# Routing logits and mean as extra columns of the value and output projections, in a fused linear-attention and mixture-of-experts kernel

## The reference, cut to what matters

```python
x = x + attn(layernorm(x))            # qkv = x @ W_attn + b ; 16 heads of 8
#   q, k = elu(.) + 1 ; causal linear attention:
#   kv_t = kv_{t-1} + k_t v_t^T ; ksum_t = ksum_{t-1} + k_t
#   y_t = (q_t kv_t) / (q_t ksum_t + eps) ; attn = y @ W_proj + b_proj
z = layernorm(x)
logits = z @ Wr + br                  # 8 experts
top two experts per token, weights = softmax over those two
out = x + sum over the two: w_e * (relu(z @ W1[e] + b1[e]) @ W2[e] + b2[e])
```

## Time and profile before

| | us |
|---|---|
| median of 3 runs (344.52 to 345.48) | 345.19 |
| profiled execution | 345.68 |
| its span, first to last instruction | 343.9 |
| busy: PE, DVE | 289.6, 275.0 |
| busy: POOL, ACT | 248.5, 224.7 |

### The profile page before, as it was taken

One profiled execution on the slowest core, in us unless ns is written; L12 is line 12 of the kernel. 1 busy time (PEld: TensorE's weight loads), 2 busy tenths in 40 slices (PEclk: granted clock), 3 DMA queues, 4 the chain that ended last, 5 costly groups with the idle time before them and its releaser, 6 DMA issues.

```text
span 343.9 us, 7875 instructions
## 1 busy us (share of the span) xinstructions
PE 289.6 (84%) x2234; PEld 207.3 (60%) x2237; DVE 275.0 (80%) x623; ACT 224.7 (65%) x654; POOL 248.5 (72%) x252
## 2 busy tenths in 40 slices
PE   4798999989989999899695799999999999995000
PEld 4587855545545555555453577688888898884000
DVE  5888899999978987997999279986777777773096
ACT  2588721469989855555408896688888888882091
POOL 4648999659999998877775577777777777777200
PEclk9699999999999999999879699999999999999655
DMA  8991000000000001011110364516445645511497
GB/s 226 352 286 47 0 2 0 0 4 0 1 0 2 0 15 43 31 53 50 42 51 33 78 110 103 104 56 102 110 104 105 117 99 104 98 56 53 134 381 240
DMA packets 50026, 29.16 MB, mean 85 GB/s; under 512 B 34993, under 2 KB 44639, under 8 KB 49986
## 3 DMA queue, kind: packets, MB, share of 16 engines
q1 hardware_dynamic: 45142, 19.02, 22.6%
q0 software_dynamic: 4544, 9.38, 9.4%
q10 hardware_dynamic: 300, 0.27, 0.3%
HBM read 10.87 MB, written 12.67 MB: 68 GB/s over the span
## 4 chain that ended last, share of the span: by engine, by line
PE 43%; DVE 19%; ACT 12%; POOL 10%; issue 10%; DMA 4%; SPq 1%; ACTq 0%; POOLq 0%; DVEq 0%
POOL y_rows L566 10%; PE ps L1286 9%; PE ps L1285 6%; PE ps L1259 4%; DVE nd L934 3%; ACT xs L682 3%; DMA qk<-y_rows 3%; PE ps L1449 2%; PE ps L1261 2%; PE ps L1451 2%; PE ps L1450 2%; PE ps L1468 2%; PE ps L1473 2%; PE ps L1469 2%; ACT junk L661 2%
## 5 line engine op out<-in xcount | busy, mean ns | idle before, releaser
L566 POOL DMA_INDIRECT y_rows<-kvt,yid x78 | 74.7, 957 | 23.8 <-issue 22.3
L534 POOL DMA_INDIRECT x_rows<-rows,pos_i x64 | 62.4, 974 | 21.3 <-issue 17.4
L740 ACT ACTIVATE ps<-ps,b1s 128x256 f32<-128x256 f32 x156 | 60.1, 448 | 16.9 <-PE ps L1451 16.2
L1171 DVE TENSOR_TENSOR wraw<-ps,wraw 128x1024 f16<-128x1024 f32 x39 | 47.8, 1225 | 19.9 <-ACT wraw L746 19.6
L1449 PE MATMUL ps<-wraw,w1h 128*128 128x256 f16 x156 | 43.4, 278 | 0.5 <-issue 0.4
L1451 PE MATMUL ps<-wraw,w1l 128*128 128x256 f16 x156 | 43.1, 276 | 0.0
L1450 PE MATMUL ps<-wraw,w1h 128*128 128x256 f16 x156 | 43.1, 276 | 0.0
L934 DVE TENSOR_REDUCE nd<-work 128x144 f32<-128x1152 f32 x32 | 41.9, 1348 | 0.4
L923 DVE TENSOR_TENSOR work<-ps,qk 128x1024 f32<-128x1024 f32 x32 | 38.1, 1216 | 5.0 <-PE ps L1286 4.9
L1468 PE MATMUL ps<-w,wraw 128*128 x312 | 39.8, 219 | 0.0
L1469 PE MATMUL ps<-w,wraw 128*128 x312 | 39.7, 219 | 0.0
(11 more groups left out here) (250 smaller groups left out, 733.1 us busy)
## 6 DMA issues: line engine op xcount, KB each, us to landing
qk<-y_rows SPq DMA_DIRECT2D x8, 512.0 KB, 6.7
wraw<-in_L_ffn_W_dram SPq DMA_DIRECT2D x1, 2048.0 KB, 11.1
out_dram<-x SPq DMA_DIRECT2D x8, 256.0 KB, 4.3
x<-in_L_attn_x_dram SPq DMA_DIRECT2D x3, 512.0 KB, 7.2
y_rows<-kvt,yid POOLq DMA_INDIRECT x78, 2.8
x_rows<-empty SPq DMA_DIRECT2D x9, 130.0 KB, 2.8
x_rows<-rows,pos_i POOLq DMA_INDIRECT x64, 2.3
wraw<-x_rows SPq DMA_TRANSPOSE x39
```

The source lines that it names most:

```text
L534: nc.gpsimd.indirect_dma_start(out=x_rows, out_offset=bass.IndirectOffsetOnAxis(ap=pos_i[:, c, t:t + 1], axis=0), in_=rows[:, t, :], in_of ...
L566: nc.gpsimd.indirect_dma_start(out=y_rows, in_=ysb[:, n % YG, g], in_offset=None, out_offset=bass.IndirectOffsetOnAxis(ap=yid[:, n, g:g + ...
L740: ins = nc.scalar.activation(o, o, ACT.Relu, bias=b1s[:, bass.ds(e * HC + c, 1)])
L1171: nc.vector.tensor_tensor(hl[:, n % HB], inner(n), hh[:, n % HB], ALU.subtract).then_inc(lo_done, 1)
```

## The change

The normalised row is (x2 - mean) * rstd, so its product with Wr is rstd times the product of x2 with a centred Wr. Now x2 = x + y W_proj + b, so eight extra columns of W_proj (W_proj times the centred Wr) and a ninth (its negated row mean) give the part from y. The part from x comes out of the first normalisation: eight extra columns of the value projection give the centred x times Wr, divided by the first standard deviation. Both parts are added by `proj` itself, whose PSUM tile is 137 columns wide per token tile (`XW`) and not 128; the value's is 136 (`VW`). `turn_x2`, `copy_x2T`, `logits`, `copy_logits` and the row sums are gone; `choose_first` multiplies by rstd. Groups become `[5, 5, 3, 3]`, chosen two iterations after their last unit (`ROUTE = 2`): in iterations 6, 11 and 14, and the last after the loop. The first table is begun in iteration 11 and not 13. `statistics` and `norm_2` come one iteration earlier, the scales and casts move to iterations 0 to 6, and the lists of the loop are re-dealt.

```diff
+    LW = E + 1
+    XW, VW = D + LW, D + E
-    GROUPS = [3, 4, 3, 3, 3]
+    GROUPS = [5, 5, 3, 3]
-    FIRST = 3
+    FIRST = 2
+    ROUTE = 2
+    TABLE_AT = G_LAST[FIRST - 1] + ROUTE
-    EARLY_Y = 2
-    CASTS = {**{s: (3, 3) for s in range(2, 7)}, 7: (2, 0)}
-    LOWS = {3: 3, 4: 3, 5: 3, 6: 3, 7: 3, 8: 1}
+    CASTS = {0: (4, 2, 6), 1: (0, 2, 2), 3: (0, 2, 2), 4: (0, 2, 2), 5: (0, 2, 2), 6: (0, 2, 2)}
+    LOWS = {0: 4, 1: 1, 2: 3, 3: 2, 4: 2, 5: 2, 6: 2}
-    KV_AT = {0: (6, 7), 2: (8,), 3: (9,), 4: (10,), 5: (11,), 6: (12,), 7: (13,), 8: (14,), 10: (15,)}
+    KV_AT = {0: (6, 7), 1: (8,), 2: (9,), 3: (10,), 4: (11,), 5: (12,), 6: (13,), 10: (14,), 11: (15,)}
-    X_AT = {8: 2, 9: 5, 10: 5, 11: 6, 12: 6, 13: 4, 14: 9, 15: 3}
+    X_AT = {7: 5, 8: 5, 9: 5, 10: 5, 11: 2, 12: 6, 13: 6, 14: 6}
+    X_LATE = (2, 2)
...
# GpSimd, loop
-                if s >= 2:
-                    power_2(s - 2)
+                if s >= 1 and s < U - 1:
+                    power_2(s - 1)
+                for u in KV_AT.get(s, ()):
+                    kv_products(u)
                 for n in range(low, low + LOWS.get(s, 0)):
                     weights_low(n)
...
# ScalarE, loop
-                nc.scalar.activation(x[:, t], ps[:, 7, a * P:(a + 1) * P], ACT.Copy, accum_out=sums[:, t:t + 1])
+                nc.scalar.activation(tiles(x, u), ps[:, 7, 0:TPU * XW].rearrange("p (a d) -> p a d", a=TPU), ACT.Copy
...
+                for n in range(cast, cast + first):
+                    cast_weights(n)
                 copy_yT(s)
-                if s >= 1:
-                    statistics(s - 1)
+                for n in range(cast + first, cast + first + between):
+                    cast_weights(n)
                 copy_x2(s)
-                if s >= 2:
-                    norm_2(s - 2)
+                statistics(s)
+                if s >= 1:
+                    norm_2(s - 1)
...
# after the loop, ScalarE
+            hidden(0)
             norm_2(U - 1)
-            hidden(0)
-            copy_x2T(U - 1)
             hidden(1)
-            copy_logits(NG - 1)
# VectorE, new in iteration 0
+            def logit_parts():
+                dve.wait_ge(rstd_done, LOADS)
+                link(nc.vector.reciprocal(lnt[:, 0, :], rstd[:, 0, :]))
+                link(nc.vector.tensor_tensor(ps_parts, v[:, :, D:VW], lnt[:, 0, :].unsqueeze(2).broadcast_to([P, NT, E]), ALU.mult))
+                dve.wait_ge(fold_out, 4)
+                nc.vector.tensor_tensor(logits, ps_parts, b_fold[:, 0:E].unsqueeze(1).broadcast_to([P, NT, E]),
+                                        ALU.add).then_inc(parts_done, 1)
+                nc.vector.tensor_scalar(mean, lnt[:, 3, :], b_fold[:, E:LW], None, ALU.add).then_inc(parts_done, 1)
...
+                dve.wait_ge(x2_done, G_LAST[g] + 1)
+                dve.wait_ge(rstd2_done, G_LAST[g] + 1)
+                link(nc.vector.tensor_tensor(logit, logits[:, gt], rstd[:, 1, gt].unsqueeze(2).broadcast_to([P, n, E]), ALU.mult))
...
# VectorE, before the first block
             y_rows_of(0)
+            split_low(U - 2)
+            choose_first(NG - 1)
+            choose_second(NG - 1)
             y_rows_of(1)
+            positions(NG - 1)
+            counts(1)
# TensorE, front
+            def fold(k):
...
+                    nc.tensor.matmul(ps_fold[0], centre[:, :], wr[:, :], start=True, stop=True).then_inc(fold_done, 1)
+                    nc.tensor.transpose(ps_fold[1], wproj[:, 0:D], ident[:, :]).then_inc(fold_done, 1)
+                    nc.tensor.matmul(ps_fold[2], junk[:, 0], w_fold, start=True, stop=True).then_inc(fold_done, 1)
+                    nc.tensor.matmul(ps_fold[3], bproj[:, :].broadcast_to([P, P]), w_fold, start=True,
...
# TensorE, loop
-                if s >= 3:
-                    turn_x2(s - 3)
                 if s + 1 < U:
                     prefix(s + 1, 1)
-                elif s >= 3:
-                    logits(s - 3)
...
# TensorE, after the loop
-            ranks(FIRST)
-            turn_x2(U - 3)
-            logits(U - 3)
-            turn_x2(U - 2)
             up(0)
-            logits(U - 2)
-            turn_x2(U - 1)
             up(1)
-            logits(U - 1)
+            ranks(NG - 1)
```

More of the change, by code:

```diff
@@ L210, in block_kernel @@
         ps_iota = scratch(E)
-        ps_br = scratch(E)
+        ps_sc = scratch(10)
         ps_lg = scratch(MOST, E)
-        ps_others = scratch(MOST, E)
         ps_second = scratch(MOST, E)
         ps_xs = ps[:, 5, 0:TPU * D].rearrange("p (a d) -> p a d", a=TPU)
+        ps_parts = ps[:, 5, TPU * D:TPU * D + NT * E].rearrange("p (t e) -> p t e", e=E)
+        xd, mean, logits = x[:, :, 0:D], x[:, :, D + E], x[:, :, D:D + E]
+        w_fold = wqkv[:, 3 * D:3 * D + LW]
+        ps_fold = [ps[:, 7, 0:E], ps[:, 7, 0:P], ps[:, 7, 0:LW], ps[:, 7, P:P + LW]]
+        ps_wall = ps[:, 6, T + P:T + P + 3]
+        b2s, b2f = (ps[0:E, 5, TPU * D + k * D:TPU * D + (k + 1) * D] for k in range(2))
         def kv_home(u):
@@ L267, in block_kernel @@
         w2_in = sem("w2_in")
-        small_in = [sem(f"small_in{g}") for g in range(7)]
+        small_in = [sem(f"small_in{g}") for g in range(8)]
         const_done = sem("const_done")
@@ L568, in scatter_y @@
                                                  ).then_inc(y_scattered[n % YG], 16)
-            for n in range(sent, TOP * T1):
+            assert sent == TOP * T1
+            last_group = TOP * TPU * G_U0[NG - 1]
+            for n in range(sent, sent + X_LATE[0]):
                 scatter_x(n)
-            last_group = TOP * TPU * G_U0[NG - 1]
             power_2(U - 2)
-            scatter_x(TOP * T1)
+            for n in range(sent + X_LATE[0], sent + sum(X_LATE)):
+                scatter_x(n)
             power_2(U - 1)
-            for n in range(TOP * T1 + 1, last_group):
+            for n in range(sent + sum(X_LATE), last_group):
                 scatter_x(n)
-            for n in range(EARLY_Y):
-                scatter_y(n)
             for n in range(last_group, SCATTERS):
                 scatter_x(n)
-            for n in range(EARLY_Y, NBLK):
+            for n in range(NBLK):
                 scatter_y(n)
@@ L674, in norm_2 @@
                 act.wait_ge(shift2_done, u + 1)
[L675 to L676 removed]
+                if u in (0, U // 2):
+                    last = max(w for w in range(U) if KV_HOME[w] == f"rows{u // (U // 2)}")
+                    act.wait_ge(pfx_done, (last + 1) * TPU)
                 if u >= 4:
                     act.wait_ge(xl_done, u - 3)
[L679 removed]
                 for a in range(TPU):
                     t = u * TPU + a
[L682 removed]
+                    ins = nc.scalar.activation(xs[:, u % 4, a], xd[:, t], ACT.Identity, bias=shift[:, 1, t:t + 1],
                                                scale=rstd[:, 1, t:t + 1])
@@ L720, in _ @@
                     nc.scalar.activation(b1s[:], b1T[:], ACT.Copy, scale=sc[:, 17:18]).then_inc(b1s_done, 1)
-                if s >= 2:
-                    norm_2(s - 2)
-                for n in range(cast + between, cast + between + behind):
+                if s >= 1:
+                    norm_2(s - 1)
+                for n in range(cast + first + between, cast + first + between + behind):
                     cast_weights(n)
-                cast += between + behind
+                cast += first + between + behind
             regs = [act.alloc_register(name=f"act_expert{j}") for j in range(2)]
```

354 lines of the change are left out of this document (160 added, 194 removed).

## The result

The changed kernel takes 350.69 us (median, 350.35 the shortest) against 345.31 for the kernel before in the same session; the ratio is 1.0157 (95% interval 1.0134 to 1.018). It is 5.4 us slower where 6.8 us faster was forecast. The profiled execution took 350.35 us, its span is 348.6. Of the four executions three took 350.35 to 350.93 us and one, of which there is no trace, 356.85.

A forecast was written before the change was run, and what follows sets the result against it. GpSimd was taken as the bound of the expert stage, TensorE close behind. Their ends, 314.0 and 313.8, put the later one 6.8 before 320.8: profiled execution 345.68 to 338.9, median 338.4, range 334.0 to 344.8.

The forecast's parts named there:

- What bounds the kernel: GpSimd's DMA stream bounds the whole expert stage, TensorE close behind; a gain at GpSimd alone is worth at most 1.9 us.
- TensorE in the loop: A TensorE loop iteration falls from 8.14 to 7.07 us, taken as 7.1 against VectorE's 6.7.
- VectorE in the loop: VectorE sets the loop's pace; 6.1 us of waits go, new instructions come, y(15) ends at 184 to 185 instead of 185.32.
- the front: Ahead of the loop, folding instructions, extra value columns and two constants add 1.3 us, between 0.5 and 2.5.
- GpSimd up to the 40th scatter: GpSimd's waits in the loop fall from 11.2 to 5.9 us, so the 40th scatter ends at 181.3 instead of 186.56.
- GpSimd after it: After the 40th scatter, 102 DMAs and two powers end at 311.4 to 314; a late last power leaves a 2.5 us hole.
- the parity: In the loop, the y(15) time at which the change neither gains nor loses: about 193.
- Rival C: TensorE's low clock is on the loop's path every time: 14 us on y(15), to 199; median 351; chance 0.12.
- Experts: First expert block at 188.4, 5.3 earlier; block 3 5.1 earlier; last group's choice hidden; TensorE's side ends at 313.8.
- A: GpSimd alone rules the end and its loop waits shrink to 2 us instead of 5.9; median 334.5; chance 0.14.
- B: Low TensorE clock and VectorE's long loop lists leave a gain of 2 to 3; median 342.5 to 344.5; 0.24 with D.
- D: Removed work was off the path, late casts keep the 40th scatter near 186; median 343.5; chance 0.24 together with B.

The follow-up runs named there:

- e10: Changed kernel with one PSUM operand in `logit_parts` and the choices, table in SBUF with no GpSimd product beside it, scatters re-dealt; 343.43 us, 0.9928 of the kernel before.
- e1_early: Changed kernel with GpSimd's products 14 and 15 moved to iterations 8 and 9, scatters in their place; 401.79 us, no ratio could be given.
- e7: e6 with the table's running sum reading its input from PSUM, result in SBUF; third run 343.94 us, 0.9958 of the kernel before.
- e12_again: Second run of e10 plus transposes that nobody reads where TensorE stands in the loop; 343.41 us.
- e13: e12_again's kernel with the last group's choice between VectorE's halves of blocks 0 and 1, one `scatter_y` pair before that group's scatters; 340.77 us, 0.9859 of the kernel before.
- e6: Changed kernel with operands in PSUM at `logit_parts`, the first multiplication of choices 0 to 2 and the first table; 0.965 of the kernel before.
- e8_late: Changed kernel with the last power behind eight late scatters and not four; 0.967 of the kernel before, 0.972 the second time, both in long sessions.
- long sessions: Three of the seven sessions, in which every kernel, the one before too (407 to 411 us), took some 48 to 66 us longer.
- a_after: The changed kernel again, unaltered, run beside variants in one of the long sessions; 0.975 of the kernel before.
- e9_again: Second run of the edits of e7 and e8_late together on the changed kernel; 343.05 us, 0.9945 of the kernel before.

## Why the prediction was wrong, step by step

**What bounds the kernel: right.** The end is GpSimd's work plus its waits: 4.5 us more of waits, 4.7 later.

**TensorE in the loop: right.** 7.07 forecast, 7.08 measured; VectorE's five waits for prefixes are down to 0.3.

**VectorE in the loop: this step failed.** It said 184.8 for the end of y(15), which is at 196.53, and it priced every new instruction by a row of the same size: `logit_parts` at 1.5 by the quotient's 0.42, the multiplication at 0.24, the table parts as "only move". The size was not what those rows had in common: the quotient reads one operand from PSUM, and the choices of the kernel before worked in PSUM. The new ones read two from SBUF, or go from SBUF to SBUF with a scalar, and three of the five stand where the new deal puts a product. Measured: 4.1 for `logit_parts` (1.4 in e10, where it is not held, so the 1.5 was a right price for the work alone), 1.07 and 2.80 for the multiplication, 3.49 for a table instruction that had been 0.29. The product's length, 4.2 us, stood in the trace of before, and so did each operand's place in the code; I asked what each instruction costs and not what runs beside it.

The Trainium skill, "SBUF — State Buffer", section "Who interferes with whom", states the rule: VectorE with two SBUF inputs, or in a mode that uses both its ports, and a GpSimd instruction reading SBUF share one interface, and the second to start blocks. The traces agree (1.69 and 0.43 us for the same work), and go further: at 154.37 the product is two instructions of 2.1 us and VectorE stood for both, and in e1_early it stood through what was left of one and all of the next four.

Of the 11.7 us by which the forecast missed y(15), operands in PSUM give back 6.7 (e7), and the rest of the table's hold and the new order 1.9 more (e10). What is left in e10 is 3.2. There y(0) ends 1.3 earlier than forecast (59.86 for 61.2; the front costs 0.7, the first multiplication starting at 48.2 for 47.6, and not 1.3), and the way from there to y(15) is 4.5 longer. VectorE waits 4.7 us on it, 2.2 for ScalarE's copies of the normalised rows, 1.9 for the table's spread and 0.6 for a power, where the sum had 1. So this term was too small as well.

**GpSimd up to the 40th scatter.** Forecast 181.3, measured 191.1. Product 9 was right (2.4; 2.3). The last low half was said to wait 2.7 with y(6) ending at 108.8; it ended at 111.4 and the wait was 4.9, 2.2 more. (The three waits of the forecast sum up to 6.0, not 5.9.) The 4.5 before power 12 was not foreseen: y(12) is late by the two holds just ahead of it, and its variance is ready 5.9 behind its end, where the forecast had counted 3.4 for y(15). In e12_again, with the clock full, that distance is 3.9, so by estimate 2 us of this wait are the low clock.

**GpSimd after it.** Power 15 starts 4.6 behind the end of y(15) (201.09 and 196.53; 4.6 in e7_third too), not 3.4, so this term was 1.2 too small, and the parity, "y(15) at about 193", came out too late. e7_third ends y(15) at 189.9 and is 1.5 us faster than the kernel before, the changed kernel ends it at 196.5 and is 5.4 slower; by a line between the two the parity is at about 191.3, an estimate. Rival C's time, 351, was met by luck: it has y(15) at 199, and 196.5 cost as much already. Its mechanism, the clock, is not what made the loss: e7 changes no work of TensorE and gains all of it back, and with the clock full e12 gains nothing over e10. The power's wait, "if that is 187, a hole of 2.5", came as 3.74 with 196.

**Experts.** The last choice ahead of block 0 was called hidden. In the changed kernel the first copy is 15.7 behind the end of y(15), as forecast (15.8), with TensorE waiting 4.1 for `picked`. What that place costs shows once y(15) is early: 2.6 us between e12 and e13, which also moves one pair of `scatter_y`. So the forecast of 338.4 needed a second thing that this change doesn't have.

**Rivals.** A, B and D did not come about. None of them, nor C, had the real mechanism.

## What to carry to other kernels

When an instruction is added to VectorE, write down where its operands are and what GpSimd does at that moment, before its size. One operand in PSUM, or a GpSimd order without long multiplies there, made 1.69 us into 0.43 and 3.49 into 0.16 to 0.26. The length of a hold can't be counted on either: the same instruction of the same list took 1.69 in one execution and 10.01 in another. If only one instruction is cured, look at the next one with two SBUF operands, the hold goes there. And when the main term is cured, look for the next queue: here the last choice ahead of the first block.

## What the runs showed that I had not expected

A held instruction doesn't always get in behind the product beside it. L1045 began 0.7 us into a pair of products of 2.1 us each and ended with the second; the scan in e6 stood 3.98 us; L889 stood 10.01 us in e1_early and 10.02 in e8_late, up to the end of the last product. But L893 ended at 57.12, behind the first of its pair, and L889 took 1.68 to 1.70 us in the four other traces that leave it as it is in the changed kernel. What decides between the two stays open.

In the long sessions the order turns: a_after 400.02 us against 410.82 for the kernel before. There a block took (370.41 - 232.64) / 38 = 3.63 us for 2.87, which is 29 us over 38 steps, and the first copy stood 37.2 behind y(15) for 16.1, 21 us more, with a wait of ScalarE of 22.1 that names no engine; several others of 2 to 12 us don't either. The expectations from e9_again on speak of scatters that land in 3.8 us and set the pace. That was misread: 3.8 is the landing of the nine transfers that fill `x_rows` at the start (L397; 3.1 in the changed kernel's first trace), and the traces of the long sessions hold no landing of a scatter at all. So what is slow there is not known. The same chip gave e7 393.24 us in one session and 343.94 in the next. I have no profile of the kernel before from such a session, so why it suffers more there stays open.
